# Selective scan: VectorE multiplies with the spread row of B straight from PSUM

## What is computed

```python
x_dbl = hidden_states @ x_proj_w.T            # dt_r, Bmat, Cmat
delta = jax.nn.softplus(dt_r @ dt_proj_w.T + dt_proj_b)
def step(h, inp):
    u_t, delta_t, B_t, C_t = inp
    dA  = jnp.exp(delta_t[:, :, None] * A)                      # A = -exp(A_log)
    dBu = (delta_t * u_t)[:, :, None] * B_t[:, None, :]
    h   = dA * h + dBu
    y_t = jnp.einsum('bdn,bn->bd', h, C_t)
    return (h, y_t)
...
return y + u * D
```

## Time and profile before

| what | us |
|---|---|
| median of three runs | 1976.91 |
| lowest and highest of them | 1967.4 and 1982.37 |
| span of the profiled execution (first to last instruction) | 1978.3 |
| the loop of the scan in that execution, first multiplication to last scan's end | 50.5 to 220.6 |

### The profile page before, as it was taken

One profiled execution on the slowest core, in us unless ns is written; L12 is line 12 of the kernel. 1 busy time (PEld: TensorE's weight loads), 2 busy tenths in 40 slices (PEclk: granted clock), 3 DMA queues, 4 the chain that ended last, 5 costly groups with the idle time before them and its releaser, 6 DMA issues. The chain is left out here.

```text
span 1978.3 us, 35429 instructions
## 1 busy us (share of the span) xinstructions
PE 1700.6 (86%) x10848; PEld 1360.9 (69%) x10848; DVE 1418.9 (72%) x2841; ACT 993.1 (50%) x2176; POOL 707.0 (36%) x610
## 2 busy tenths in 40 slices
PE   2656599969999989998999998898699999888986
PEld 1222288847777778876777777766488888787755
DVE  6999766687888456678787756655588888757643
ACT  3443233347777434337777753211378888733211
POOL 1676422226666102214566521200155555403000
PEclk8777699979999989998999998999899999998999
DMA  0000011110000011102000003298310000003885
GB/s 28 0 0 0 22 48 43 32 51 20 19 19 8 1 31 48 48 19 65 17 21 24 6 1 109 68 257 243 112 30 27 29 29 21 1 25 93 240 241 154
DMA packets 39478, 111.15 MB, mean 56 GB/s; under 512 B 5504, under 2 KB 23664, under 8 KB 32240
## 3 DMA queue, kind: packets, MB, share of 16 engines
q1 hardware_dynamic: 39408, 110.26, 19.3%
HBM read 109.19 MB, written 1.05 MB: 56 GB/s over the span
## 5 line engine op out<-in xcount | busy, mean ns | idle before, releaser
L1298 POOL TENSOR_TENSOR xn<-xn 128x512 f32<-128x512 f32 x138 | 179.2, 1298 | 268.3 <-DVE xn L1193 268.3
L1284 POOL TENSOR_SCALAR prob<-prob,recip 128x256 f32<-128x256 f32 (+2 forms) x256 | 229.5, 911 | 70.7 <-DVE recip L1177 70.5
L1088 ACT ACTIVATE prob<-banks,peak 128x256 f32<-128x256 f32 (+3 forms) x384 | 190.2, 501 | 109.0 <-DVE peak L1168 102.9
L937 PE MATMUL banks<-pt,v 128*128 128x256 f32 (+3 forms) x768 | 204.7, 410 | 6.9 <-ACT pt L1023 6.9
L937 PEld LDWEIGHTS banks<-pt,v 128*128 128x128 f32 x768 | 145.5, 191 | 73.9 <-issue 32.1
L892 PE MATMUL banks<-k_hi,q_hi 128*128 128x256 f32 (+2 forms) x384 | 152.9, 398 | 27.0 <-DVE k_lo L1184 26.9
L1168 DVE TENSOR_REDUCE peak<-banks 128x1 f32<-128x256 f32 (+3 forms) x384 | 161.0, 446 | 18.5 <-PE banks L896 16.0
L572 POOL TENSOR_TENSOR gu_lo<-gu,gu_hi 128x512 fp32r<-128x512 f32 x36 | 46.7, 1297 | 296.8 <-ACT gu_hi L530 296.8
L282 PE MATMUL acc<-term,ident 128*128 128x512 f32 x128 | 90.6, 870 | 70.2 <-POOL term L239 70.2
L913 PE MATMUL banks<-ident,prob 128*128 128x128 f32 x864 | 140.4, 279 | 3.2 <-DVE pt L1021 3.2
L239 POOL TENSOR_TENSOR term<-state,cs 128x1024 f32<-128x1024 f32 x32 | 117.6, 3693 | 67.8 <-DVE state L402 45.2
(11 more groups left out here) (253 smaller groups left out, 5300.6 us busy)
## 6 DMA issues: line engine op xcount, KB each, us to landing
wgu<-in_w_gu SPq DMA_DIRECT2D x32, 1408.0 KB, 15.2
wd<-in_w_d SPq DMA_DIRECT2D x32, 704.0 KB
gu<-in_w SPq DMA_DIRECT2D x36, 256.0 KB, 2.7
wd<-in_w SPq DMA_DIRECT2D x36, 128.0 KB, 2.0
wkv<-in_mha_kv SPq DMA_DIRECT2D x16, 256.0 KB, 2.6
wq<-in_mqa_q SPq DMA_DIRECT2D x16, 128.0 KB, 2.1
wo<-in_mqa_o SPq DMA_DIRECT2D x16, 128.0 KB, 2.2
wq<-in_gqa_q SPq DMA_DIRECT2D x16, 128.0 KB, 2.1
```

The lines of the kernel that those rows point to most:

```text
L937: last = pe.matmul(o_bank[:, x * P:to], v[:, s, x, at:at + P], pt[:, s, x, first:first + to - x * P], start=(j == 0), stop=(j == NQ - 1))
L1088: last = act.activation(prob[:, s, cols[t]:cols[t] + n], s_bank[gi][:, psum_col[t]:psum_col[t] + n], ACT.Exp, bias=peak[:, s, t:t + 1], ac ...
L1284: last = pool.tensor_scalar(part, part, recip[:, s, t:t + 1], None, ALU.mult)
L1298: pool.tensor_tensor(cosed[:, r % 2, :], cosed[:, r % 2, :], swap[:, r % 2, :], ALU.add) \
```

## The change

ScalarE's copy of B to `bs` goes, and the buffer with it. VectorE multiplies `du` with `wide[:, 0]` in PSUM. The two multiplications now stand ahead of the wait for `decay` and the memset. `spread` is counted for B and C apart (`spread_b`, `spread_c`); B's place is free again when both multiplications of a state are done (`driven`), C's when ScalarE has copied it (`copied`, now one per state). TensorE spreads one state ahead instead of two.

```diff
-                        wait(pool, c["copied"], 2 * (k + 1), i, 4)
+                        wait(pool, c["copied"], k + 1, i, 2)
...
-            def spread(i, k):
+            def spread(i, n):
 
                 for which in range(2):
-                    wait(pe, c["copied"], 2 * k - 1 + which, i, 4)
+                    if which == 0:
+                        wait(pe, c["driven"], NC * n, i, 2 * NC)
+                    else:
+                        wait(pe, c["copied"], n, i, 2)
...
-                    last.then_inc(c["spread"].sem, 1)
+                    last.then_inc(c["spread_c" if which else "spread_b"].sem, 1)
...
             spread(0, 0)
-            spread(0, 1)
-            with pe.Fori(0, N_STATE // 2 - 1) as i:
+            with pe.Fori(0, LAST) as i:
                 for k in range(2):
-                    spread(i, k + 2)
+                    spread(i, k + 1)
                     add_terms(i, k)
-            add_terms(N_STATE // 2 - 1, 0)
-            add_terms(N_STATE // 2 - 1, 1)
+            spread(LAST, 1)
+            add_terms(LAST, 0)
+            add_terms(LAST, 1)
...
-                    for which, to in enumerate((bs, cs)):
-                        wait(act, c["spread"], 2 * k + which + 1, i, 4)
-                        if which == 0:
-                            wait(act, c["state"], 2 * k - 2, i, 4)
-                        else:
-                            wait(act, c["read"], 2 * k - 2, i, 4)
-                        act.activation(to[:, k, :], wide[:, which, :], ACT.Copy).then_inc(c["copied"].sem, 1)
+                    wait(act, c["spread_c"], k + 1, i, 2)
+                    wait(act, c["read"], 2 * k - 2, i, 4)
+                    act.activation(cs[:, k, :], wide[:, 1, :], ACT.Copy).then_inc(c["copied"].sem, 1)
...
+                    wait(dve, c["spread_b"], k + 1, i, 2)
+                    for dc in range(NC):
+                        wait(dve, c["state"], 2 * k + dc - 3, i, 4)
+                        dve.tensor_tensor(drive[:, k, dc, :], du[:, dc, :], wide[:, 0, :], ALU.mult) \
+                            .then_inc(c["driven"].sem, 1)
                     wait(dve, c["decay"], 2 * (k + 1), i, 4)
-
                     dve.memset(decay[:, k, :, 0:T:SEQ], 0.0).then_inc(c["zeroed"].sem, 1)
-                    wait(dve, c["copied"], 2 * k + 1, i, 4)
-                    for dc in range(NC):
-
-                        wait(dve, c["state"], 2 * k + dc - 3, i, 4)
-                        dve.tensor_tensor(drive[:, k, dc, :], du[:, dc, :], bs[:, k, :], ALU.mult) \
-                            .then_inc(c["driven"].sem, 1)
                     wait(dve, c["zeroed"], k + 1, i, 2)
```

More of the change, by code:

```diff
@@ L184, in selective_scan @@
         ("size", 0), ("relu", 0), ("nega", 0), ("e", 0), ("lg", 0), ("over", 0), ("main", 0),
-        ("ready", 0), ("spread", 0), ("copied", 2), ("decay", 0), ("driven", 0), ("state", 4),
+        ("ready", 0), ("spread_b", 0), ("spread_c", 0), ("copied", 0), ("decay", 0), ("driven", 0), ("state", 4),
         ("read", 4), ("summed", 4), ("gated", 0), ("turned", 0), ("zeroed", 0), ("selected", 0), ("added", 0))}
@@ L204, in selective_scan @@
         sbuf(nc, "term", [P, 2, NC, T], F32) as term,
-        sbuf(nc, "bs", [P, 2, T], F32) as bs,
         sbuf(nc, "cs", [P, 2, T], F32) as cs,
@@ L264, in _ @@
             pe.wait_ge(c["selected"].sem, 1)
-            def spread(i, k):
+            def spread(i, n):
                 for which in range(2):
-                    wait(pe, c["copied"], 2 * k - 1 + which, i, 4)
+                    if which == 0:
+                        wait(pe, c["driven"], NC * n, i, 2 * NC)
+                    else:
+                        wait(pe, c["copied"], n, i, 2)
                     for s in range(NSEQ):
-                        n = 2 * i + (k + which * N_STATE)
-                        at = slice(n, n + 1) if isinstance(i, int) else bass.ds(n, 1)
+                        row = 2 * i + (n + which * N_STATE)
+                        at = slice(row, row + 1) if isinstance(i, int) else bass.ds(row, 1)
                         lhs = pick[:, at, :].rearrange("p o m -> p (o m)")
@@ L287, in _ @@
             pe.wait_ge(c["relu"].sem, 2)
+            LAST = N_STATE // 2 - 1
             spread(0, 0)
-            spread(0, 1)
-            with pe.Fori(0, N_STATE // 2 - 1) as i:
+            with pe.Fori(0, LAST) as i:
                 for k in range(2):
-                    spread(i, k + 2)
+                    spread(i, k + 1)
                     add_terms(i, k)
-            add_terms(N_STATE // 2 - 1, 0)
-            add_terms(N_STATE // 2 - 1, 1)
+            spread(LAST, 1)
+            add_terms(LAST, 0)
+            add_terms(LAST, 1)
             for t in range(NT):
@@ L329, in _ @@
             act.wait_ge(c["ready"].sem, NC)
-            act.sem_inc(c["copied"].sem, c["copied"].prime)
             with act.Fori(0, N_STATE // 2) as i:
```

## The result

The changed kernel takes 1951.33 us in the median of four runs (1939.39 to 1958.17), the kernel before 1977.8 us (four runs); the ratio is 0.986, with a 95% interval of 0.981 to 0.990. Two later comparisons of the same two kernels gave 0.9836 (0.979 to 0.988) and 0.9828 (0.978 to 0.988). The forecast was 1942 us, 1930 to 1954, and faster by more than 1%.

The account below looks back on a forecast made before the run. The prediction took turn-taking between VectorE's two-SBUF-operand instructions and GpSimd's products to bound the scan loop. Saving 32.1 us over 15 periods and 3.1 at the start, 35.2 in all, it forecast 1942 us, range 1930 to 1954.

Parts of the forecast that it names:

- What bounds the loop: Scan loop: VectorE's scans and multiplications with two SBUF operands take turns with GpSimd's products, making 10.9 us a state.
- The multiplication from PSUM: VectorE's multiplications reading B from PSUM run beside GpSimd's products, 2.4 to 2.6 us for two, at no cost.
- The period: Loop time per state, between ends of scan pairs: from 10.89 to 8.75 us, saving 32.1 us over 15 periods.
- the lower bound: Least loop period: the old 10.89 us less both undisturbed multiplications, 2.36 us, giving 8.53.
- The start: Loop's beginning: multiplications start at 47.1 without waiting for B's copy, first scan at some 49.65, 3.1 us earlier.
- TensorE one state ahead: TensorE's queue in the loop: B's row up to 1.2 us late, inside 1.8 us spare; cost nothing, bounds 0 to 0.3.
- the cover: GpSimd's pair of products, 4.43 us a state, under which multiplications and memset, some 2.6 us, were to lie.
- The sum: Whole program: 32.1 us from the periods and 3.1 from the start, 35.2 us saved, giving 1942 us.
- B: Rival, 13%: the scan slips in between two products, or TensorE becomes the bound; period about 9.06 us, time 1946.
- the first half of B: Loop: if GpSimd's second product begins late, the next scan, ready at 2.6 us, goes first; period 9.06 us.
- C: Rival, 13%: the multiplication, its SBUF operand first, still takes turns with GpSimd; period stays 10.89 us, time 1974.
- D: Rival, 4%: slower, VectorE's PSUM read in the multiplication held up by TensorE's PSUM writes; 1997 us at 4.05 each.

Follow-up runs that it names:

- e5: The kernel before with GpSimd's products cut to the first half of the tokens; one run of 1948.38 us, period 8.73 us a state.
- e2: The changed kernel with B copied to SBUF by ScalarE and read there again, the new order kept; ratio to the kernel before 1.0016.
- e7: The changed kernel with the scan's second operand, drive, in PSUM too, by halves of 512 tokens; 1944.63 us, ratio to the kernel before 0.984.
- e10: e8 with TensorE spreading the rows two states ahead of the additions instead of one; 1926.56 us, ratio to the kernel before 0.974.
- e8: The changed kernel with drive in PSUM in whole tiles, looping over one feature chunk after the other; ratio to the kernel before 0.998.
- e4: The changed kernel with the multiplication's two operands exchanged, PSUM first and SBUF second; one run of 1942.54 us.
- e6: The changed kernel with GpSimd's products cut to the first half of the tokens; one run of 1921.13 us, period 6.88 us a state.

## Why the prediction was right, step by step

*What bounds the loop.* Right, and shown from three sides: e5 (GpSimd shorter, VectorE's multiplications shorter), e2 (operand back, standing still back), e7 and e10 (the scan out of the exchange, no scan ever stretched). The Trainium skill says the same in "SBUF — State Buffer", section "Who interferes with whom": a VectorE instruction with two SBUF inputs contends with a GpSimd instruction that reads SBUF, and the one that comes second is blocked for the whole of the other. The traces agree, for the scan too (4.33 us at the longest with drive in SBUF, 2.29 with drive in PSUM).

*The multiplication from PSUM.* Right that it costs nothing under the products; my length was a little high. I took up to 1.28 us, the median is 1.205, no longer than the fastest from SBUF (1.218). The 65 ns for a PSUM operand, an estimate from the Trainium skill, "VectorE: DVE Perf Modes", section "The TRN2 errata", do not show at all here. The scan was ready 2.29 us after the last scan's end (98.24 to 100.53), where I had 2.6.

*The period.* 8.75 was forecast, 8.80 measured. By its terms: products 4.43 forecast, 102.70 - (91.74 + 6.50) = 4.46 measured; the two scans from GpSimd's release 2.13 + 2.19 = 4.32 forecast, 107.04 - 102.70 = 4.34 measured. Two side readings were off and moved nothing. A product alone takes 2.33 to 2.36 us, not some 2.2; the sum used the pair's 4.43 as a whole. And the lower bound's spacing, 2.36 - 1.18, should take off the 1.22 us of one multiplication, which gives 1.14 and a bound of 8.61 instead of 8.53.

*The start.* 3.1 us forecast, 3.0 measured; the multiplications begin at 47.36 where I took 47.1.

*TensorE one state ahead.* Called free with up to 1.2 us of lateness inside the cover. It was: VectorE waited for the row 0.9 us in all, twice. What I did not say is how much this rests on the cover. In e8 the spreads stand in the same order against the additions, without the standing still of the scan, and VectorE waited 42.5 us for the row there.

*The sum.* 35.2 us forecast, 34.4 measured in the loop. The time, 1942 forecast, came out at 1951.33, near the upper end of the range, and at 1944.29 and 1943.57 in the two later sets. What was sized too small is the spread: I gave a forecast made from one execution -9.5 and +5.5 us, but behind the loop the changed kernel alone takes 1751 to 1768 us from profile to profile, and one of the first four runs (1958.17) lies above my range. That the first median lies inside is therefore partly luck.

*The rivals.* B: no scan came between two products of one state in the rows shown, and TensorE (clock 0.83 in the mean) was late by 0.9 us in all. But the first half of B was closer than I had it. I took the second product to begin at 2.2 us and the scan to be ready at 2.6; the first product ended at 96.28 + 4.11 = 100.39, 2.15 us after the last scan, and the next scan was ready at 2.29. That is 0.14 us to spare, not 0.4, so that this part of the forecast was partly luck. C: excluded by e4 and by the multiplications' 1.205 us. D: excluded by the same row, whose longest is 1.220.

## What to carry to other kernels

Where VectorE is busy without a gap, compare the shortest and the median duration of each of its lines before calling it the bound: an instruction that takes 1.2 us at best and 3.3 in the median is waiting inside itself, and GpSimd's timeline beside it tells for what. Count the SBUF operands of VectorE's instructions that run beside GpSimd; one operand moved to PSUM, where the row lies anyway, freed the multiplication here and then the scan. The instruction to look at next is the one that stands still after the change. When a wait that covered other work goes, look through the in-order lists again: e8 lost everything to an order that had been free in the changed kernel.

## What was not expected of the hardware

A GpSimd product of 128x1024 takes 2.35 us undisturbed (e7, 32 times), and one of half the size 1.26 us at its shortest (e5, e6); e5's period says the same, (10.89 - 8.73) / 2 = 1.08 us less for each. TensorE's granted clock in the loop differed between kernels with the same work for TensorE. It was 0.75 in the mean before and 0.83 in the changed kernel. With twice the spreads it was 0.81 in e8 (50 to 160 us), where TensorE waited 36.2 us for GpSimd's products, and 0.95 in e10, where it waited 4.9 us for them. What raises it no run here isolates.
